# Second attention layer: the turned units and the blocks loaded back share one buffer of two places, and the diagonal blocks stay where they were written

## The reference

```
q = x @ Wq;  k, v = split(context @ Wkv)          # 16 heads x 64
dots = einsum('bhnd,bhmd->bhnm', q, k) * 64**-0.5
dots = dots - (1 - mask)[:, None, :, None] * 1e6
attn = softmax(dots, axis=-1)
out  = einsum('bhnm,bhmd->bhnd', attn, v)         # then @ Wout + bout
```

## Time and profile before

| | us |
|---|---|
| median of 3 runs | 915.78 (908.65 to 916.7) |
| time of the profiled execution | 913.91 |
| span of its trace | 912.3 |
| busy: PE / PEld / ACT / DVE / POOL | 828.5 / 734.4 / 673.3 / 638.7 / 453.2 |
| loads `PTC<-turned_blocks` | 256 of 128 KB |
| stores `turned_blocks<-BT` | 64 of 512 KB |
| bytes moved by DMA | 171.93 MB |

### The profile page before, as it was taken

How to read it: one execution, slowest core, us unless ns; L and a number is a source line. 1 busy time by engine, 2 the same in 40 slices (tenths; PEclk the granted TensorE clock), 3 DMA queues, 4 the chain that set the end, 5 groups by cost and what they waited for, 6 DMA issues and landing times.

```text
span 912.3 us, 28139 instructions
## 1 busy us (share of the span) xinstructions
PE 828.5 (91%) x7885; PEld 734.4 (80%) x7885; DVE 638.7 (70%) x2052; ACT 673.3 (74%) x2662; POOL 453.2 (50%) x765
## 2 busy tenths in 40 slices
PE   5899999999998877999999678999999999999985
PEld 3677777777776766999999577889999999999974
DVE  5888887887887743222222578788898888888872
ACT  2999899899898852333334798899888888888860
POOL 3135445444454362111113777788777777776540
PEclk9999999999999997999999899999999999999987
DMA  5897667667767702222222198889899999999871
GB/s 169 247 244 217 204 208 227 201 211 228 219 208 240 196 30 78 70 71 70 70 70 64 64 253 253 253 240 269 246 241 232 238 238 237 240 239 240 240 233 41
DMA packets 160451, 171.93 MB, mean 188 GB/s; under 512 B 16052, under 2 KB 139318, under 8 KB 160374
## 3 DMA queue, kind: packets, MB, share of 16 engines
q1 hardware_dynamic: 153474, 156.77, 60.0%
q0 software_dynamic: 6112, 13.90, 5.7%
q10 hardware_dynamic: 788, 0.39, 0.2%
HBM read 90.87 MB, written 80.13 MB: 187 GB/s over the span
## 4 chain that ended last, share of the span: by engine, by line
PE 67%; DMA 9%; issue 8%; DVE 6%; SPq 4%; POOL 3%; ACT 3%; another core or an unknown queue 0%; POOLq 0%; DVEq 0%; ACTq 0%
PE bank L1233 8%; PE bank L1420 8%; PE bank L1392 7%; PE bank L1399 7%; PE bank L1442 5%; PE bank L1516 4%; PE bank L1432 4%; PE bank L1225 4%; DMA PTC<-turned_blocks 3%; PE bank L1506 3%; PE bank L1187 3%; PE bank L1344 3%; PE bank L1304 2%; PE bank L1521 2%; ACT PR L699 2%
## 5 line engine op out<-in xcount | busy, mean ns | idle before, releaser
L699 ACT ACTIVATE PR<-PR,nmx 128x128 f32<-128x128 f32 x512 | 198.4, 393 | 13.7 <-DVE nmx L898 13.6
L699 ACT ACTIVATE PR<-bank,nmx 128x128 f32<-128x128 f32 x512 | 188.0, 432 | 0.4 <-DVE nmx L898 0.4
L347 POOL TENSOR_TENSOR PR<-PR,rden 128x512 f32<-128x512 f32 x128 | 133.1, 1052 | 50.4 <-DVE rden L903 49.8
L699 ACT ACTIVATION_READ_ACCUMULATOR PR<-bank,nmx 128x1 f32 x512 | 139.6, 273 | 0.0
L1420 PE MATMUL bank<-XCT,wqk 128*128 128x128 f32 x832 | 104.6, 280 | 10.0 <-ACT XCT L687 9.7
L793 ACT ACTIVATE H<-bank 128x512 f32<-128x512 f32 x70 | 41.8, 597 | 92.3 <-PE bank L1392 92.3
L1420 PEld LDWEIGHTS bank<-XCT,wqk 128*128 128x128 f32 x832 | 98.3, 193 | 13.5 <-ACT XCT L687 10.5
L699 ACT ACTIVATION_READ_ACCUMULATOR PR<-PR,nmx 128x1 f32 x512 | 98.2, 192 | 0.0
L1187 PEld LDWEIGHTS bank<-ident,PR 128*128 128x128 f32 x512 | 60.2, 141 | 39.6 <-issue 38.1
L1065 DVE STREAM_TRANSPOSE BT<-PR 128x512 f32<-128x512 f32 x128 | 89.7, 701 | 2.3 <-POOL PR L347 1.5
L898 DVE TENSOR_REDUCE nmx<-bank 128x4 f32<-128x512 f32 x128 | 86.2, 673 | 4.5 <-PE bank L1225 3.5
(11 more groups left out here) (186 smaller groups left out, 1986.1 us busy)
## 6 DMA issues: line engine op xcount, KB each, us to landing
turned_blocks<-BT SPq DMA_DIRECT2D x64, 512.0 KB
PTC<-turned_blocks SPq DMA_DIRECT2D x256, 128.0 KB, 4.2
second_layer_values<-wide SPq DMA_DIRECT2D x32, 512.0 KB
wide<-second_layer_values SPq DMA_DIRECT2D x32, 512.0 KB
expert_outputs<-HF SPq DMA_DIRECT2D x32, 256.0 KB
expert_outputs<-HF SPq DMA_DIRECT2D x64, 128.0 KB
KBD<-expert_outputs SPq DMA_DIRECT2D x64, 128.0 KB
QS<-expert_outputs SPq DMA_DIRECT2D x32, 256.0 KB
```

The costliest lines, as they stand in the source:

```text
L347: nc.gpsimd.tensor_tensor(unit, unit, rden[:, p, G * g:G * g + G].unsqueeze(2).broadcast_to([P, G, P]), ALU.mult).then_inc(s["nm"], 1)
L699: last = nc.scalar.activation(PR[:, g, j * P:(j + 1) * P], scored, ACT.Exp, bias=nmx[:, p, h:h + 1], accum_out=den[:, p, h:h + 1])
```

## The change

`BT` becomes another name for `PTC`. A unit is turned into the place of its sequence's parity, the store reads it there, and the loads write over it. A block on the diagonal (queries r = keys j) needs no other partitions, so it is left. The four loads of a half become six: partitions j = 0 load blocks 1 to 3, j = 1 block 0 and blocks 2 to 3, j = 2 blocks 0 to 1 and block 3, j = 3 blocks 0 to 2. Of the six, two carry 96 KB, two 64 KB and two 32 KB, 384 KB instead of 512 KB. The stores still carry all blocks. The turn now waits until PE is through with the sequence two before (`pv`), where it waited for the last store; the store's wait on the loads, and the loads' wait on `pv`, go.

```
-        BT = sb("BT", [P, 2, 2 * G * P])
+        BT = PTC[:].rearrange("p a g i h b -> p a g (i h b)")
...
             def store_blocks(m, p, half):
 
-                wait_apart(sp, (c["bt"], NU * m + 2 * half + 2), (c[f"pt{half}"], 64 * (m - 1)))
-                sp.dma_start(bt_dram[p, half], BT[:, half, :]).then_inc(c[f"bw{half}"], 16)
+                wait_apart(sp, (c["bt"], NU * m + 2 * half + 2))
+                sp.dma_start(bt_dram[p, half], BT[:, p, half, :]).then_inc(c[f"bw{half}"], 16)
 
             def load_turned(m, p, half):
 
-                wait_apart(sp, (c[f"bw{half}"], 16 * (m + 1)), (c["pv"], NU * (m - 2) + 2 * half + 2))
-                for j in range(4):
-                    sp.dma_start(PTC[32 * j:32 * j + 32, p, half, :, :, :].rearrange("a i h b -> a i (h b)"),
-                                 bt_dram[p, half].rearrange("(i a) (j c) -> j a i c", a=32, j=4)[j]).then_inc(c[f"pt{half}"], 16)
+                wait_apart(sp, (c[f"bw{half}"], 16 * (m + 1)))
+                for j, low, high in ((0, 1, 4), (1, 0, 1), (1, 2, 4), (2, 0, 2), (2, 3, 4), (3, 0, 3)):
+                    sp.dma_start(PTC[32 * j:32 * j + 32, p, half, low:high, :, :].rearrange("a i h b -> a i (h b)"),
+                                 bt_dram[p, half].rearrange("(i a) (j c) -> j a i c", a=32, j=4)[j][:, low:high]).then_inc(c[f"pt{half}"], 16)
...
-                def turn_unit(m, g):
+                def turn_unit(m, p, g):
                     dve.wait_ge(c["nm"], NU * m + g + 1)
-                    wait(dve, c[f"bw{g // 2}"], 16 * m)
-                    nc.vector.transpose(BT[:, g // 2, :].rearrange("p (j h b) -> p h j b", j=4, b=32)[:, G * (g % 2):G * (g % 2) + G],
+                    wait(dve, c["pv"], NU * (m - 2) + 2 * (g // 2) + 2)
+                    nc.vector.transpose(BT[:, p, g // 2, :].rearrange("p (j h b) -> p h j b", j=4, b=32)[:, G * (g % 2):G * (g % 2) + G],
                                         PR[:, g, :].rearrange("p (h j b) -> p h j b", h=G, j=4)).then_inc(c["bt"], 1)
...
-                    wait(pe, c["pt0"], 64 * (n - 1))
+                    wait(pe, c["pt0"], 96 * (n - 1))
...
-                    wait(pe, c["pt1"], 64 * (n - 1))
+                    wait(pe, c["pt1"], 96 * (n - 1))
```

More of the change, by code:

```diff
@@ L1086, in step1 @@
                 if exists(n - 1):
-                    turn_unit(n - 1, 0)
+                    turn_unit(n - 1, q, 0)
                     sums_reciprocal(c, n - 1, q, 2)
@@ L1095, in step1 @@
                 if exists(n - 1):
-                    turn_unit(n - 1, 1)
+                    turn_unit(n - 1, q, 1)
                     sums_reciprocal(c, n - 1, q, 3)
@@ L1101, in step1 @@
                 if exists(n - 1):
-                    turn_unit(n - 1, 2)
+                    turn_unit(n - 1, q, 2)
                 if exists(n):
@@ L1105, in step1 @@
                 if exists(n - 1):
-                    turn_unit(n - 1, 3)
+                    turn_unit(n - 1, q, 3)
                 if exists(n + 3):
```

## The result

| | before | after |
|---|---|---|
| median of 3 runs, us | 915.78 (908.65 to 916.7) | 946.44 (946.42 to 946.88) |
| profiled execution, span, us | 912.3 | 944.8 |
| mean granted clock | 0.974 | 0.966 |

The ratio is 1.036, with a 95% interval of 1.028 to 1.044. On a second chip it was 1.036 again (1.032 to 1.040). The forecast was 911 us, with 924 as the range's upper end.

What follows compares the result with a forecast made beforehand. PE was taken to bound the later stretch (629 to 860), with PE, ScalarE and DMA near full in the early one. Early waits gave 913.9 - 3.6 = 910.3, later steps and end 0; forecast 911 us, range 903 to 924.

Steps and rivals of the forecast that it cites:

- Fewer bytes: Loads in each step: 0.26 MB less, 1.1 us of DMA time; in the later stretch (629 to 860) worth nothing.
- the sum: Whole kernel: 3.6 us won in five early steps (539 to 629), 0 in later steps, 0 at the end.
- More transfers: SP's queue: twelve loads for eight issue the last load 1.4 us later, bounds +1.0 and +2.1.
- The discount for small transfers: SP's issue time: loads with fewer 1 KB runs issue faster, 1.1 ns a run, saving 0.84 us over twelve loads.
- From the last issue to landing: Last load of a later step: finds the queue empty, lands 2.5 us after issue, 0.8 us earlier than before.
- Later values and first store: SP's queue: later values fit the gaps (4.0 us later, 1.5 early); store landing up to 1.4 us later counted as balanced.
- 1.1 us of relief: Early steps: time given back by 0.26 MB less in the DMA queue, set against a store landing up to 1.4 us later.
- The prediction's own signs of being wrong: Load waits in the later stretch, an early first-half store issued late behind the values, or a landing above 4 us.
- hidden anyway: Rival, chance 0.24: in early steps SP holds the next store and loads start later by their gain; 913 to 916.
- Issue-bound, slower: Rival, chance 0.15: landing does not shorten as the queue empties; 922 (0.10), or 944 (0.05) if it takes 5.4 us.
- DMA was the bound: Rival for the early steps, chance 0.15: byte relief removes all waits and the clock's dip; 901 at best, 904 with end unchanged.
- The rule of the Trainium skill on small transfers: Loads: coalesce small transfers, under 64 KB is mostly overhead; spoke against the change, landing near the late bound if overheads were serial.

Runs made afterwards that it cites:

- e3: Changed kernel, but four loads of three blocks (96 KB each) per half, eight issues; one block of two partition groups not moved: 907.02 us, 0.994 times before.
- e4: Changed kernel with twelve loads, the values' load moved behind the second half's store and ahead of the turned loads: 911.78 us, 0.998 times before.
- e10: Changed kernel with twelve loads, the values' load moved behind the next store of the first half: 910.62 us, 1.001 times before.
- e7: Kernel before with its eight loads, the values' load moved between the second half's store and the turned loads: 891.27 us, 1.008 times before.

## Why the prediction was wrong

- *Fewer bytes, nothing in the later stretch, a little in the early:* right. e3 gives 5 us where the sum had 3.6 (in its trace the first eleven steps are 3.4 us shorter), and the DMA share of the later stretch fell further than forecast, to 0.67 instead of 0.84, at 209 GB/s instead of 240.
- *More transfers, +1.4 us to the last issue:* right in the later steps (757.28 to the end of twelve less one issue is 5.1 us, where eight took 3.7), too low in the early ones, where it is 595.42 - 589.22 = 6.2 us against 3.2, because single issues took up to 1.56 us. The discount for small transfers did not exist: apart from these, 0.42 to 0.44 us each back to back, whether 96, 64 or 32 KB.
- *From the last issue to landing, 2.5 us:* right, and even a little long. The loads land 1.9 to 2.4 us after their issue (medians by size), as the queue empties; in the later stretch (KB each, us):

```profile
PTC<-turned_blocks SPq DMA_DIRECT2D x71, 96.0 KB, 2.2
PTC<-turned_blocks SPq DMA_DIRECT2D x72, 64.0 KB, 2.0
PTC<-turned_blocks SPq DMA_DIRECT2D x72, 32.0 KB, 1.9
```

- *"Later values and first store ... I count these as equal":* **this is the step that failed.** It priced the values' moving close ahead of the store once, against 1.1 us of relief, and did not follow it round. All shifts go into one loop: a later values' load delays the store's landing, this the loads, these the next values. The numbers to close it were at hand. The chain of waits of the kernel before has an early store that was issued 0.5 us behind the values:

```profile
552.08 5.60 DMA turned_blocks<-BT
```

  5.6 us to land, 12 x 0.46 = 5.5 for twelve issues and 0.95 for output and values make 12.0 us, against the 89.9 / 8 = 11.2 of an early step: a loss already. Measured are 13.1 to 14.1 us for the loop in the early stretch, of which 5.3 to 6.5 are the landing of the first half's store and 6.3 to 7.0 the twelve loads. So the sum closes the loop but is 1 to 2 us short, most of it by the long issues. The prediction's own signs of being wrong came in part: the first store right behind the values in the early steps, and waits of PE for loads behind 640. A landing above 4 us did not come.
- *The rivals:* "hidden anyway" named this place (SP holding the next store) but let the loss end at zero. "Issue-bound, slower" has 944 at its end, near the measured 946, and is not borne out: its mechanism was a landing that stays at 5.4 us, paid in 19 later steps, while these lost 1.6 us in fourteen and the landing shortened. In "DMA was the bound" the 904 should be 905 (913.9 - 7.1 - 1.8).
- *The rule of the Trainium skill on small transfers* ("DMA: Bandwidth & Descriptors", Rules for kernel authors) pointed the right way. What makes it true here is mostly the issue time on SP inside a loop: the same twelve small loads in e4 and e10 are within 0.2% of the kernel before. By their ratios they are still 0.4 and 0.7% slower than e3, which moves the same bytes in eight, so that a small cost of the further transfers stays.

What stays open: why single issues take 1.3 to 1.6 us, which makes up some 1 us of the early loop, and why the second half's stores take 6.8 us to land in the early stretch and 5.2 in the later one. No run took the loads' own backlog away alone. That two changes of the order (e4, e10) restore the time to the same 0.2% doesn't say that the loop has the same length in both.

## What to carry to other kernels

When a queue's program has a wait on its own earlier transfer, add up the loop: landing, every issue, whatever else is issued, back to the transfer. Compare that sum with the step; below it the issues are free, above it each one is paid in every step. And look at what is issued right ahead of a transfer whose landing is waited for: 512 KB that nobody needs soon cost here 3.6% with twelve loads in the loop, and one place in the order gave them back. With eight loads, where the loop seldom bound, moving them ahead of the loads cost 0.8% instead (e7).

## What the runs showed of the hardware

On SP, most issues back to back took 0.42 to 0.45 us for 32, 64, 96 and 128 KB alike (32 to 128 runs of 1 KB), and the first load behind a wait 0.32 us (589.22 above). Some issues lasted 1.3 to 1.6 us, the one at 593.82 above among them; what stretched them is not shown. A store of 512 KB, issued 0.5 us behind a load of 512 KB, landed after 5.3 to 6.5 us, and after at most 2.9 to 3.8 us with that load behind it (e10). The kernel before had medians of 884 us on one chip and 910 to 916 on others.
